# A third row buffer, stage-sized pacing memsets, transposed logits and another split of the result copies in a fused adaLN + mixture-of-blocks kernel

## The reference

```python
h = gelu(x @ W.T + fc_bias + lowrank(x, v, u) + cond)     # rank 16, v = u = the side input of the batch
prob = softmax(h @ w_router + b_router)                   # 16 blocks
mask = top_k(prob, 4)                                     # 4 of 16 blocks for each token
y = sum over the chosen blocks e of relu(h @ w1[e].T + b1[e]) @ w2[e]   # each block 128 wide
out = x + y + b2
```

## Time and profile before

| | us |
|---|---|
| median of 3 runs (1144.09 to 1147.14) | 1146.56 |
| the profiled execution | 1149.37 |
| its span, first to last instruction | 1147.6 |
| rows and tiles together (steps 32 to 63) | 197 to 587 |
| tiles alone | 600 to 933 |
| final sums | 936 to 1147.6 |

### The profile page before, as it was taken

The page is one execution under the profiler, slowest core; times in us unless marked ns, Lnnn a source line. Parts: engine busy times, 40 slices in busy tenths (PEclk is TensorE's granted clock), DMA queues, the critical chain, the costliest instruction groups (busy, mean ns, idle before and its releaser), DMA issues.

```text
span 1147.6 us, 18685 instructions
## 1 busy us (share of the span) xinstructions
PE 865.1 (75%) x4893; PEld 682.7 (59%) x4893; DVE 861.7 (75%) x2175; ACT 581.1 (51%) x1061; POOL 727.4 (63%) x1038
## 2 busy tenths in 40 slices
PE   8989989999999999999999876999999930000000
PEld 7757767777777776777777655788888820000000
DVE  4556666777687767767778974878998759987777
ACT  6535545756676575657657753766667610000000
POOL 1588888888888888888888897555555530000000
PEclk9989989999999999999999997999999965555555
DMA  6798679988899888988778887689987589999999
GB/s 188 262 330 299 236 270 334 310 293 298 288 314 305 289 285 300 312 282 297 265 276 313 302 289 262 245 296 342 317 282 243 192 313 425 425 427 429 426 432 378
DMA packets 103241, 354.88 MB, mean 309 GB/s; under 512 B 29961, under 2 KB 29961, under 8 KB 92384
## 3 DMA queue, kind: packets, MB, share of 16 engines
q1 hardware_dynamic: 59616, 217.22, 55.0%
q0 software_dynamic: 43424, 136.37, 30.3%
q10 hardware_dynamic: 96, 0.10, 0.0%
HBM read 200.47 MB, written 169.65 MB: 323 GB/s over the span
## 4 chain that ended last, share of the span: by engine, by line
PE 50%; DVE 14%; POOL 12%; DMA 11%; issue 7%; ACT 3%; another core or an unknown queue 2%; ACTq 0%; POOLq 0%; DVEq 0%; SPq 0%
PE lay L1185 12%; DMA w2l<-yt 9%; PE yps L1327 9%; PE hid L1294 8%; PE trn L1279 7%; POOL yt L563 4%; POOL xg L544 4%; PE hid L1299 4%; POOL w2l L528 3%; DVE stx L1040 3%; PE hid L1171 2%; PE trn L1206 2%; ACT gsb L643 2%; DMA outT<-ys 2%
## 5 line engine op out<-in xcount | busy, mean ns | idle before, releaser
L544 POOL DMA_INDIRECT xg<-grow,ix x224 | 226.7, 1012 | 70.2 <-issue 36.4
L817 DVE TENSOR_TENSOR gsb<-trn,gsb 128x512 fp32r<-128x512 f32 x239 | 162.4, 687 | 127.3 <-ACT gsb L643 75.2
L563 POOL DMA_INDIRECT yt<-ys,ids x170 | 176.7, 1039 | 72.6 <-issue 35.8
L1185 PE MATMUL lay<-w2l,xs 128*128 128x512 f32 x768 | 194.3, 403 | 0.0
L1279 PE MATMUL trn<-idf,gr 128*128 128x128 f32 x956 | 147.3, 277 | 27.0 <-DVE gsb L817 12.9
L1185 PEld LDWEIGHTS lay<-w2l,xs 128*128 128x128 f32 x768 | 144.6, 192 | 30.1
L528 POOL MEMSET w2l<- 128x320 f32 x412 | 161.3, 392 | 0.1
L1279 PEld LDWEIGHTS trn<-idf,gr 128*128 128x128 f32 x956 | 115.8, 142 | 68.3 <-DVE gsb L817 22.9
L643 ACT ACTIVATE gsb<-trn 128x512 fp32r<-128x512 f32 x239 | 142.6, 597 | 26.5 <-PE trn L1279 15.2
L1294 PE MATMUL hid<-gsb,w1c 128*128 128x512 f32 (+1 forms) x576 | 133.1, 374 | 11.9 <-ACT gsb L643 10.2
L671 ACT ACTIVATE hv<-hid,b1c 128x512 f32<-128x512 f32 (+1 forms) x94 | 52.6, 584 | 155.4 <-PE hid L1299 53.0
(11 more groups left out here) (243 smaller groups left out, 1823.9 us busy)
## 6 DMA issues: line engine op xcount, KB each, us to landing
gr<-xg SPq DMA_DIRECT2D x49, 1056.0 KB
xs<-yt SPq DMA_DIRECT2D x16, 2048.0 KB, 19.5
w2l<-yt SPq DMA_DIRECT2D x15, 2048.0 KB, 19.5
gr<-xg SPq DMA_DIRECT2D x45, 528.0 KB
stx<-xT SPq DMA_DIRECT2D x64, 256.0 KB, 4.3
outT<-ys SPq DMA_DIRECT2D x31, 512.0 KB, 20.4
xg<-xrow SPq DMA_DIRECT2D x16, 528.0 KB
w2f<-xrow SPq DMA_DIRECT2D x16, 512.0 KB
```

The source lines that it names most:

```text
L544: pool.indirect_dma_start(out=xg, out_offset=bass.IndirectOffsetOnAxis(ap=ix[:, row_buffer(b), q, k:k + 1], axis=0), in_=grows[row_buffer( ...
L563: pool.indirect_dma_start(out=yt, out_offset=bass.IndirectOffsetOnAxis(ap=ids[:, j % 8, c:c + 1], axis=0), in_=yss[result_buffer(j)][:, c, ...
L817: dve.tensor_tensor(gsb[:, :, LO, c * P:(c + 1) * P], turned[TURN_BANK[n]][:, :].rearrange("p (k t) -> p k t", k=KC), gsb[:, :, HI, c * P: ...
L1185: pe.matmul(lay[s % 2][:, :], xs[:, b % 2, k, h, cols], wls[:, k, a, :], start=(k == 0 and a == HI and h == HI), stop=False)
```

## The change

- `row_buffer(b)` is `b % 3` throughout; the third buffer `grow3` lies in `w2l` from block 11 on. `uw`, `zs`, `vw` move to blocks 8 to 10.
- `yspare` is gone. Result buffers are five: 0 and 1 alone for tiles below 34, then `grow[1]` (batch 13's, from tile 34), `stx` (from 36), `grow[0]` (batch 15's, from 39). Tile 39 is the first user of `grow[0]`.
- POOL sends before it scatters in steps 33 to 66, and scatters first in the others. Before, it scattered first except where `s % 4` is 3.
- The pacing memsets are 160 columns in steps 7 to 31, 288 in steps 32 to 63, 160 after; from step 69 on they write `fu`. `stop` is left out for tiles 69 to 71.
- `presplit_w2` runs in steps 67 to 74, blocks in order. Block 15 waits for POOL's step 68, block 11 for the last scatter out of `grow3`.
- `turn_logits` is four PE transposes of 128x128; `choose` adds the four chunks with one more DVE reduction. `sumk` and its five POOL instructions are gone.
- ACT copies chunks 0, 1 and 2 of tiles 34 to 46, DVE chunk 3.
- SP issues the load of `b2` one step later (81) and waits for the last paced memset first.

```diff
-MORE = 36, 39, 43, 55
+MORE = 34, 36, 39, 55
-REST = 320
+REST = 160, 288, 160
+DUMP = SLOTS + 5
+THREE = 34, 47
 def row_buffer(b):
-    return b % 3 if b < 6 else b % 2
+    return b % 3
...
-        free = [0, 1] + [2] * (j <= SPARE) + [3] * (j >= MORE[0])
-        free += [4] * (MORE[1] <= j < MORE[3]) + [5] * (MORE[2] <= j < MORE[3])
+        free = [0, 1] + [2] * (MORE[0] <= j < MORE[3]) + [3] * (j >= MORE[1]) + [4] * (MORE[2] <= j < MORE[3])
...
+def by_act(j, c):
+    return c % 2 == 0 or c == 1 and THREE[0] <= j < THREE[1]
...
-        yss = (ys[:, 0, :, :], ys[:, 1, :, :], yspare, stx, grow[:, 0, :, 0:D], grow[:, 1, :, 0:D])
+        yss = (ys[:, 0, :, :], ys[:, 1, :, :], grow[:, 1, :, 0:D], stx, grow[:, 0, :, 0:D])
...
-                if s == SLOTS + 16:
+                if s == SLOTS + 17:
+                    sp.wait_ge(g_pace, 4 * SLOTS + 4 * (PACED - LAG - 2))
...
-                idle = w2l[:, NE - 1, 0:REST].bitcast(F32) if s < SLOTS + 7 else rep[:, :, :].rearrange("p q e -> p (q e)")
+                n = REST[0] if s < LAG + 2 else REST[1] if s < SLOTS else REST[2]
+                idle = w2l[:, NE - 1, D - n:D].bitcast(F32) if s < DUMP else fu[:, 0:n]
...
-                elif c == 1:
+                elif c == 1 and j < NTILE - 3:
                     stop()
...
-                first = s <= LAG + 2 or q != 3
+                first = s <= LAG + 2 or SLOTS + 3 <= s
...
-                elif result_buffer(j) > 3:
-                    b = NB - 6 + result_buffer(j)
+                elif result_buffer(j) > 1:
+                    b = NB - 5 + result_buffer(j)
                     for q in range(4):
                         act.wait_ge(s_sc[row_buffer(b)][q], rows_sent(b))
-                if j == 1:
-                    for q in range(4):
-                        act.wait_ge(s_sc[2][q], rows_sent(5))
...
-                lgs = rps[:, 256:256 + 4 * NE].rearrange("p (q e) -> p q e", q=4)
+                lgs = lexp
+                step(dve.tensor_reduce(lgs[:, :, :], rps[:, :].rearrange("p (q k e) -> p q e k", q=4, k=KC)[:, :, 0:NE, :],
+                                       AX.X, ALU.add))
...
                 if e == NE - 1:
-                    dve.wait_ge(g_pace, 4 * SLOTS + 4 * (SLOTS + 5 - LAG))
-                if e == 8:
-                    dve.wait_ge(s_y[2], results_sent(max(j for j in range(NTILE) if result_buffer(j) == 2)))
+                    dve.wait_ge(g_pace, 4 * (DUMP - 7) + 4 * (DUMP - LAG - 2))
+                if e == 11:
+                    for q in range(4):
+                        dve.wait_ge(s_sc[2][q], rows_sent(NB - 2))
...
-                    last = pe.matmul(rps[:, 256 + q * NE:256 + (q + 1) * NE], lgT[:, q * P:(q + 1) * P], sumk[:, :],
-                                     start=True, stop=True)
+                    last = pe.transpose(rps[:, q * P:(q + 1) * P], lgT[:, q * P:(q + 1) * P], idf[:, :])
```

More of the change, by code:

```diff
@@ L31 @@
 PRE = 46
-SPARE = 40
-MORE = 36, 39, 43, 55
+MORE = 34, 36, 39, 55
 FOUR = 42
@@ L109, in result_buffer, with copies @@
     return RESULT_BUFFER[j]
[L112 to L117, removed]
+def by_act(j, c):
+    return c % 2 == 0 or c == 1 and THREE[0] <= j < THREE[1]
+def copies(j, c):
+    return sum(by_act(i, k) == by_act(j, c) for i in range(j + 1) for k in range(chunks(i)) if (i, k) <= (j, c))
 def results_sent(j):
@@ L291, in adaln_ffn @@
         s_sc = [[sem(f"s_sc_{n}_{q}") for q in range(4)] for n in range(3)]
-        s_y = [sem(f"s_y_{n}") for n in range(6)]
+        s_y = [sem(f"s_y_{n}") for n in range(5)]
         s_yin = [sem(f"s_yin_{n}") for n in range(len(yin))]
@@ L435, in _ @@
                 if s == SLOTS + 16 + 8:
-                    for n in (4, 5):
+                    for n in (2, 4):
                         sp.wait_ge(s_y[n], results_sent(max(i for i in range(NTILE) if result_buffer(i) == n)))
@@ L514, in _ @@
             pool.iota(order[:, :], [[1, 2]], base=0, channel_multiplier=2).then_inc(g_k, 1)
[L515 to L519, removed]
             paced = [0]
@@ L557, in send @@
             def send(j, c):
-                if c % 2 == 0:
-                    pool.wait_ge(a_y, 2 * j + c // 2 + 1)
+                if by_act(j, c):
+                    pool.wait_ge(a_y, copies(j, c))
                 else:
-                    pool.wait_ge(v_y, 2 * j + c // 2 + 1)
+                    pool.wait_ge(v_y, copies(j, c))
                 pool.indirect_dma_start(
@@ L728, in _ @@
                     split_w2(j - 1, expert[j - 1][0])
-                for n in presplit_in(s):
-                    presplit_w2(PRESPLIT[n])
+                if SLOTS + 3 <= s < SLOTS + 3 + NE // 2:
+                    for e in range(2):
+                        presplit_w2(2 * (s - SLOTS - 3) + e)
                 if s == KC + 1 or q == 2 and 2 <= b <= NB:
@@ L756, in _ @@
                         take_tile(j + 1, c)
-                    if s <= SLOTS and 0 <= j - 1 and c % 2 == 0 and c < chunks(j - 1):
+                    if s <= SLOTS and 0 <= j - 1 and by_act(j - 1, c) and c < chunks(j - 1):
                         result(j - 1, c)
@@ L761, in _ @@
                     if s > SLOTS and 0 <= j - 1 and j != NTILE - 1 and c in (2, 3) and 2 * c - 4 < chunks(j - 1):
+                        if c == 3 and by_act(j - 1, 1):
+                            result(j - 1, 1)
                         result(j - 1, 2 * c - 4)
@@ L1016, in result @@
                     dve.wait_ge(p_r, SLOTS // 2)
-                elif result_buffer(j) > 3:
-                    b = NB - 6 + result_buffer(j)
+                elif result_buffer(j) > 1:
+                    b = NB - 5 + result_buffer(j)
                     for q in range(4):
                         dve.wait_ge(s_sc[row_buffer(b)][q], rows_sent(b))
-                if j == 1 or (j == 0 and c == 3):
-                    for q in range(4):
-                        dve.wait_ge(s_sc[2][q], rows_sent(5))
                 dve.tensor_copy(yss[result_buffer(j)][:, c, :], second_out[RESULT_BANK[4 * j + c]][:, :]).then_inc(v_y, 1)
@@ L1125, in _ @@
                         take_tile(j + 1, c)
-                    if c % 2 == 0 and presplit_in(s):
-                        presplit_w2(presplit_in(s)[c // 2])
-                    if s <= SLOTS and 0 <= j - 1 and c % 2 == 1 and c < chunks(j - 1):
+                    if SLOTS + 3 <= s < SLOTS + 3 + NE // 2 and c % 2 == 0:
+                        presplit_w2(2 * (s - SLOTS - 3) + c // 2)
+                    if s <= SLOTS and 0 <= j - 1 and not by_act(j - 1, c) and c < chunks(j - 1):
                         result(j - 1, c)
@@ L1135, in _ @@
                             hidden(j)
-                        if 0 <= j - 1 and c < chunks(j - 1):
+                        if 0 <= j - 1 and c < chunks(j - 1) and not by_act(j - 1, c):
                             result(j - 1, c)
```

32 lines of the change are left out of this document (15 added, 17 removed).

## The result

The changed kernel takes 1176.16 us (median of 4 runs, 1169.71 to 1181.51) where the kernel before took 1146.76 beside it: ratio 1.0259, 95% interval 1.0203 to 1.0316. It is 2.6% slower, where 1142 us and 0.4% faster had been forecast; the range ended at 1153. Its profiled execution took 1169.71 us.

The account below looks back on a forecast made before the run. The loop of PE, ACT and DVE was taken to set the pace, POOL close behind, with POOL's chain after 600 us. Gains of 3.2 us to tile 46 and 1.3 at the end, 4.5 together, gave 1142 us; range 1133 to 1153.

Parts of the forecast that it names:

- the memset term of steps 7 to 31: Steps 7 to 31: 100 shorter POOL pairs, 12.7 us, mostly not gained because the other loop sets the pace.
- the loop of PE, ACT and DVE sets the pace here, with POOL close behind it: Rows and tiles together, 197 to 587 us: this loop paces 31 steps, 390 us, 12.58 us a step.
- One of my signs: Sign of being right: POOL idle for results between 200 and 587 us by some 10 us or more.
- The other sign: Sign of being wrong: steps before 587 us taking under 12.3 us would mean POOL held them.
- Memsets: POOL's pacing memsets: 265 ns (160 columns), 367 (288); 12.7 and 6.4 us mostly not gained, 7.1 us on POOL's critical stretch.
- the third rival: POOL held the earlier stages after all, so memset savings come out of the loop: 1134 us, chance 0.15.
- The first rival: PE's unascribed 10.8 us stop, seen in steps 73 and 74, returns after tile 39's stall: 1153 us, chance 0.2.
- The pair doesn't get shorter: Second rival: POOL's pairs keep their length, so the last scatter starts 6.1 us later: 1148 us, chance 0.12.
- Transposed logits and row buffer: Before step 64: logits 3 us faster, third row buffer costs 1.5 us; together the tile loop comes 4.5 us earlier.
- Tile 39's wait: Tile 39's first copy waits for batch 15's scatters in POOL's step 70: about 16 us, until 671.9.
- The end: Last tiles: 1.3 us less without `stop` before a third chunk; b2's later load costs 0.

Follow-up runs that it names:

- b_first160: The kernel before with 160 instead of 320 memset columns in steps 7 to 31, nothing else; 1175.26 us, ratio 1.0238.
- b_mid288: The kernel before with 288 memset columns in steps 32 to 63 alone; 1142.27 us, ratio 0.9941.
- after_again: The changed kernel, untouched, measured once more in another session; 1111.58 us, ratio 0.9836 to the kernel before.
- b_last384: The kernel before with 384 memset columns in steps 64 to 70 alone; 1133.98 us, ratio 1.0023.
- a_all320: The changed kernel with 320 memset columns everywhere; 1140.85 us, ratio 1.0094 to the kernel before.
- a_first320: The changed kernel with the memsets of steps 7 to 31 back at 320 columns; 1155.15 us, ratio 1.0068 to the kernel before.
- b_logits_again: The kernel before with the transposed logits alone, measured once more; 1148.59 us, ratio 1.0000.
- a_both320: The changed kernel with 320 memset columns in steps 7 to 31 and from step 64 on; 1142.52 us, ratio 0.9970 to the kernel before.
- a_late43: The changed kernel with 320 columns before step 32 and from 64, batch 15's buffer given out from tile 43; 1154.40 us, ratio 1.0028 to the kernel before.
- b_last160: The kernel before with 160 memset columns in steps 64 to 70 alone; 1166.01 us, ratio 1.0134.

## Why the prediction was wrong

The step that failed is the memset term of steps 7 to 31 ("mostly not gained", put at nothing): shorter memsets there cost 23.9 us to step 32 in the result and 28.6 us of the median by themselves (b_first160). Behind it stands a second wrong step, the loop that was taken to set the pace.

*What bounds the kernel.* The step "the loop of PE, ACT and DVE sets the pace here, with POOL close behind it" failed. I took the engine that PE's waits named (DVE, 9.1 us) over the one without slack. POOL's own rows said it: 345.9 us busy and, before 122 scatters, 19.7 us of issue gaps; the sends add 20.0, and POOL's waits for results, indices and tables 4.4, which together fill the 390. b_mid288 (-6.4 us for 256 x 0.023 = 5.9 us of POOL) and session C (29.3 for 30.9, of the sum over all stages) show it. One of my signs came true all the same: POOL waits for results in the middle stretch of after, 10.1 us, as this row of its groups shows.

```profile
L562 POOL DMA_INDIRECT yt<-ys,ids x124 | 126.1, 1017 | 31.1 <-issue 20.0 <-ACT ys L698 10.1 <-DMA tabi<-table 0.7
```

It doesn't tell who holds the loop. The other sign did: a step took 381.5 / 31 = 12.31 us in after, at the bound of 12.3 that I had set for "POOL held them", and 11.87 in after_again.

*Memsets.* The durations were right: 253 to 266 and 369 ns where I took 265 and 367. What they are worth was wrong on both sides of zero. "Mostly not gained" is false without late signals: the third rival (POOL held the earlier stages) was the right mechanism, and bigger than I gave it. The whole change gained 12 us to step 32 (185.1 against b_last384's 197.1) and 15 in the middle; against a_all320, where only the memsets differ, it is 9.0 and 16.1. With late signals the same term costs: +23.9 us to step 32 in the result, and in b_first160 `gelu(32)` came at 229.1 us, 35.7 later than in a_first320 beside it. I had bounded it by zero and by a gain and never by a loss, although nothing in a row excluded one. This is the term that turned the sign.

*The unascribed stop.* The first rival asked the right question at one place. I took the 10.8 us of the earlier trace rows for something that a stop of PE brings on at steps 73 and 74. In truth ACT stood for 49.9 us behind late signals in 45 to 720 us of the kernel before (first line of the table), and what makes them more in the stretches without tiles or without rows is the shorter memsets of POOL. In the middle stretch the sums don't order the two widths: 12.6 us with 288 columns in after, 24.7 with 320 in before. The sentence that spoke against the rival, that no engine is shown to wait for POOL's work there, is true and misled me: no wait for POOL is involved.

*The pair doesn't get shorter.* Refuted where DMAs follow one another: a DMA every 1.38 us, with 0.97 us for its descriptors. The lock that the Trainium skill describes ("SBUF — State Buffer", "SBUF: two separate sides") took nothing back here: the mean scatter took 1004 ns after and 1011 before over the span, 985 and 1017 in the middle stretch.

*Transposed logits and row buffer.* The added reduction took 0.42 us, as estimated; the 3 us for the logits were 0 within 2.4 us (b_logits_again), which fits POOL holding the stretch. The 1.5 us of the row buffer weren't measured by themselves.

*Tile 39's wait.* The mechanism and its place were right and its size too small. Where no late signals hide it, it is ACT's longest wait after 600 us, ended by a scatter, with PE standing 24 us behind it; from after_again, then a_both320:

```profile
644.94 0.60 ACT L698 ACTIVATE grow<-yps 128x512 f32<-128x512 f32 x1 [23.07 <-DMA xg<-grow,ix]
```

```profile
670.53 0.60 ACT L698 ACTIVATE grow<-yps 128x512 f32<-128x512 f32 x1 [24.12 <-DMA xg<-grow,ix]
```

I had 671.9 for its end and 16 us for its length; from the start of POOL's last scatter (642.09 in after_again) to the copy it was 2.9 us, where I took 5.5. From there to tile 46 it was 55.5 and 57.5 us, predicted 58.3 and 3 more for the clock. The sum was thus 4 to 6 us too long there. In the result itself PE was late anyway: POOL's last scatter and the copy of tile 39 in after are

```profile
692.00 0.97 POOL L543 DMA_INDIRECT xg<-grow,ix  x1 [0.16 <-issue]
```

```profile
701.38 0.59 ACT L698 ACTIVATE grow<-yps 128x512 f32<-128x512 f32 x1
```

against a forecast of 666.4 for the first: it was 26 us later, 24 of them from ahead of step 32. What the wait costs by itself stays partly open. In C the way from step 63 to tile 46 took 156.7 us in a_all320 and 142.6 in b_last384, 14 us more, which is all of the edits there together, a_all320's wider memsets of steps 71 to 76 among them. With batch 15's buffer given out from tile 43, this way took 135.5 us in a_late43, the shortest of all, against 150.2 and 148.0 of a_both320's code in other sessions; but a_late43 as a whole was no faster than the kernel beside it (1.0028), and where 160 columns made signals late nothing was left of the gain (159.2 and 160.1 in D; 1.0174 and 1.0234, the intervals overlap). An undisturbed session wasn't met again, so the price of this wait isn't shown.

*The end.* From the first copy of tile 71 (929.4 and 950.9) to the last instruction: 218.2 us before, 217.0 after, 1.2 less where 1.3 was forecast. No wait of DVE for a memset is left among the presplits, as forecast.

*What stays open.* Why a session has late signals and of what degree, and what in the chip holds PE's signals. The amount of DMA traffic doesn't separate them: in 80 to 100 us the DMA share was 0.82 with late signals (after) and 1.02 without (after_again), and in both traces the last packet of a POOL DMA ended on average 2 to 4 us behind its descriptors. That the shorter memsets are the cause of the loss is shown; the way from them to PE's signals isn't.

## What to carry to other kernels

When the chain of waits has pieces that it gives to nobody, sum the waits with that mark over the whole span, on the engine behind, before calling them local; and bound an edit that makes an engine's DMAs denser by a loss too. An engine without slack sets the pace even when no wait names it: add up its busy time and its issue gaps against the stretch. And measure an edit of pacing in more than one session: the same kernel was 2.6% slower and 1.6% faster than the same baseline, and the wide distance of 320 columns, which costs 29 us in the undisturbed session, kept the baseline between 1130 and 1151 us everywhere, while the changed kernel went from 1112 to 1176. Of the versions run, the kernel before with 288 columns in steps 32 to 63 beats both kernels in the session where it was measured (0.9941); session E's 417.2 us for 288 columns warn that it needn't hold.

## What the runs showed of the hardware that was not expected

- PE's signals can come long after its last record that could have given them (11.2 us in after, 14.0 in b_last160), several in a bunch within 0.14 us, while ACT's and POOL's come within 0.01 us and the latest of DVE's 1.7. The profile shows it as waits for "remote" or "another core", although one core runs.
- How much it costs grows as POOL's indirect DMAs get closer. Starts 1.38 us apart ahead of step 32 cost 21 to 36 us in S, A, D and E and nothing in C. 1.50 (0.97 + 0.37 + 0.16) in the middle stretch did no harm in four of the six sessions; in B and E the stretch took 17 to 35 us more than the 382 of A. Even at 1.52 the kernel before was 16 to 21 us slower outside C.
- The traces with late signals hold 19 to 31% fewer signal events of PE than those without (603 to 699 against 866 to 869), so sums of waits by their releaser come out too small in them.
- The condition changed on one chip within half an hour: 1146.64 and 1150.85 us for the kernel before in A and B, 1130.28 in C.
